# One image's scan moved into the sampling stage of a four-layer convolution kernel, 448 columns at a time

## The reference, cut to what matters

```python
# third layer: deformable convolution, 9 taps, 4 corners each
py = base_y + kh + dy;  px = base_x + kw + dx          # dy, dx from a 3x3 convolution
y0 = floor(py); x0 = floor(px); wy = py - y0; wx = px - x0
sampled = v00*(1-wy)*(1-wx) + v01*(1-wy)*wx + v10*wy*(1-wx) + v11*wy*wx   # v: gathered pixels
sampled = sampled * mask
out = einsum('bkhwc,ock->bohw', sampled, w2)

# fourth layer: selective scan over the pixels of an image, 128 channels, 16 states
def step(h, inp):
    dt_t, B_t, C_t, u_t = inp
    dA = exp(dt_t[..., None] * A)
    h = dA * h + (dt_t * u_t)[..., None] * B_t[:, None, :]
    return (h, einsum('bdn,bn->bd', h, C_t))
```

## Time and profile before

| | us |
|---|---|
| median of 3 runs | 6257.39 |
| lowest and highest run | 6249.47 to 6259.31 |
| span of the profiled execution, first to last instruction | 6244.6 |
| the median stands over that span by | 12.8 |
| busy PE / DVE / ACT / POOL in the span | 4411.3 / 5012.8 / 2533.4 / 4904.1 |
| sampling stage, first to last gather issue | 885.6 to 3119.0 |
| first memset of the scan stage | 3167.9 |
| mean granted TensorE clock, as a share of 2.4 GHz | 0.81 |

### The profile page before, as it was taken

The page is one execution under the profiler, slowest core; times in us unless marked ns, Lnnn a source line. Parts: engine busy times, 40 slices in busy tenths (PEclk is TensorE's granted clock), DMA queues, the critical chain, the costliest instruction groups (busy, mean ns, idle before and its releaser), DMA issues. The chain is left out here.

```text
span 6244.6 us, 55481 instructions
## 1 busy us (share of the span) xinstructions
PE 4411.3 (71%) x14922; PEld 2398.8 (38%) x14922; DVE 5012.8 (80%) x3958; ACT 2533.4 (41%) x3949; POOL 4904.1 (79%) x3492
## 2 busy tenths in 40 slices
PE   3777656565555657463338888888888888888887
PEld 1566523332323233232214444444444444444443
DVE  5899736776766676666639999999999999999998
ACT  2222111111111111110026666666766766766664
POOL 1777627777777777777719999999999999999997
PEclk8887766656565656655569999999999999999999
DMA  6666623444434443443324544454454544444443
GB/s 165 133 135 136 139 79 104 123 114 145 123 104 133 127 123 105 135 116 114 104 79 149 165 157 154 161 162 148 160 163 147 169 151 156 160 153 162 155 152 120
DMA packets 379240, 855.17 MB, mean 137 GB/s; under 512 B 195672, under 2 KB 238576, under 8 KB 374580
## 3 DMA queue, kind: packets, MB, share of 16 engines
q1 hardware_dynamic: 294228, 619.96, 33.3%
q0 software_dynamic: 84672, 231.32, 12.4%
HBM read 768.83 MB, written 56.48 MB: 132 GB/s over the span
## 5 line engine op out<-in xcount | busy, mean ns | idle before, releaser
L863 POOL DMA_INDIRECT fl_quad<-table,fl_idx x1764 | 1697.3, 962 | 695.0 <-issue 536.7
L2097 POOL TENSOR_TENSOR ma_hc<-ma_h,ma_cc 128x784 f32<-128x784 f32 x1024 | 1882.2, 1848 | 235.8 <-DVE ma_h L1998 203.7
L1642 PE MATMUL ma_bank<-ma_hc,ident 128*128 128x392 f32 x4096 | 1528.0, 495 | 10.2 <-POOL ma_hc L2097 7.6
L1998 DVE TENSOR_TENSOR_SCAN ma_h<-ma_da,ma_state,ma_bank 128x784 f32<-128x784 f32 x768 | 1418.0, 1846 | 101.6 <-DVE ma_bank L1985 3.5
L1014 DVE TENSOR_TENSOR fl_part<-fl_quad,fl_bank 128x2304 f32<-128x2304 f32 x196 | 500.1, 2552 | 710.1 <-DMA fl_quad<-table,fl_idx 696.6
L1867 ACT ACTIVATE ma_da<-ma_dt,ma_a_neg 128x784 f32<-128x784 f32 x1024 | 948.2, 943 | 271.1 <-DVE ma_h L1998 176.6
L1985 DVE TENSOR_TENSOR ma_bank<-ma_dtu,ma_bank 128x784 f32<-128x784 f32 x1024 | 983.4, 960 | 80.5 <-PE ma_bank L1629 79.1
L1155 PE MATMUL fl_bank<-ident,fl_tap 128*128 128x128 f32 (+1 forms) x980 | 242.3, 409 | 937.4 <-DVE xres L1032 876.0
L1642 PEld LDWEIGHTS ma_bank<-ma_hc,ident 128*128 128x128 f32 x4096 | 705.3, 189 | 449.5 <-POOL ma_hc L2097 36.0
L1022 DVE TENSOR_REDUCE fl_tap<-fl_part 128x576 f32<-128x2304 f32 x196 | 796.5, 4064 | 0.1
L1629 PE MATMUL ma_bank<-ma_bc,ma_sel 96*128 96x512 bf16 (+1 forms) x2048 | 514.8, 333 | 376.2 <-DVE ma_h L1998 361.0
(11 more groups left out here) (229 smaller groups left out, 6131.6 us busy)
## 6 DMA issues: line engine op xcount, KB each, us to landing
ma_cc<-c_rows SPq DMA_DIRECT2D x512, 784.0 KB, 4.3
mx_win<-flat SPq DMA_DIRECT2D x64, 878.0 KB, 10.3
fl_quad<-table,fl_idx POOLq DMA_INDIRECT x1764, 2.7
table<-fl_xt SPq DMA_DIRECT2D x64, 392.0 KB
mx_mask<-in_c_mask SPq DMA_DIRECT2D x56, 294.0 KB, 4.5
ma_xs<-ma_x SPq DMA_DIRECT2D x64, 196.8 KB, 5.6
ma_xs<-ma_x SPq DMA_DIRECT2D x64, 196.5 KB, 6.1
mx_xf<-flat SPq DMA_DIRECT2D x8, 816.0 KB, 15.8
```

The lines of the kernel that those rows point to most:

```text
L863: gp.indirect_dma_start(quad[i][:, kk, :], None, table, bass.IndirectOffsetOnAxis(ap=idx[i][:, kk:kk + 1], axis=0))\
L1642: ins = pe.matmul(ps_y[:, t, :], ident[:], hc[:, n % RH, at], start=False, stop=(n == DS - 1))
L1998: dve.tensor_tensor_scan(h[:, i % RH, :], da[:, i % RH, :], ps_bu[i % 2], before, ALU.mult, ALU.add).then_inc(scand, 1)
L2097: gp.tensor_tensor(hc[:, i % RH, :], h[:, i % RH, :], cc[:, i % (NGRP * GRP), :], ALU.mult)\
```

## The change

Image 0's fourth layer leaves the scan stage, which now goes through seven images (`NLITE` = 1, `NBM` = `NB - NLITE`), and is done inside the sampling stage. It is cut into 7 pieces of 448 columns, which with the two branches make 14 sections (`NSECT`) of 16 units, 224 units. `units(T)` gives slot T its units: none before `FIRST` = 59, then 5 units in 3 slots (`RATE`), so one or two in a slot, up to slot 193. GpSimd does none of it: `times_c` is now VectorE's, and C is spread by TensorE into PSUM (`spread_c`), as B is. Beside the units run a section's preparation and output (`chain`), on TensorE, ScalarE and VectorE, and before the first unit `set_up` (slot 3) and `intro` (slots 54 to 58).

Room is made for it. `RQ` is 3, `part` is one buffer and not two, `xres` holds two pairs and not four, and in PSUM convolution chunks, offset chunks and transposes share one bank (`cps`, `xps`, `tps`), so each waits until the one before was read; `turn_x` moves behind `turn_offsets`. `stage_norm3` is gone: `normal` takes each pair's statistics in the first slots of the next pair, and the last pair's behind the last tile. The weights of the scan are loaded in this stage by 26 more transfers on SP's queue. The tensor_reduce over the corners (`corners`) is as before, on all tiles.

```diff
@@ constants
+NLITE = 1
+LC = 448
+NLC = PIX // LC
@@ stage_flow
-    RQ = 4
+    RQ = 3
+    NSECT = 2 * NLC * NLITE
+    NUNIT = DS * NSECT
+    INTRO = NSEQ + 5
+    PERSLOT = 3
+    NINTRO = 13
+    FIRST = INTRO + (NINTRO + PERSLOT - 1) // PERSLOT
+    RATE = (5, 3)
...
-        part = [s_.sb(f"part{i}", [TS, 4, K2, CH]) for i in range(2)]
+        part = s_.sb("part", [TS, 4, K2, CH])
...
-        cps = [bank[:, 4 + i, :] for i in range(2)]
-        xps = bank[0:2 * PW, 6, 0:7 * CH].rearrange("p (a c) -> p a c", c=CH)
-        tps = bank[:, 7, 0:HT * M].rearrange("p (a m) -> p a m", m=M)
+        cps = bank[:, 2, :]
+        xps = bank[0:2 * PW, 2, 0:7 * CH].rearrange("p (a c) -> p a c", c=CH)
+        tps = bank[:, 2, 0:HT * M].rearrange("p (a m) -> p a m", m=M)
+        cof = bank[:, 3, 0:4 * K2]
+        ps_b, ps_c, ps_y, ps_f = (bank[:, 4 + i, 0:LC] for i in range(4))
...
+        def units(T):
+            lo, hi = ((T + i - FIRST) * RATE[0] // RATE[1] for i in range(2))
+            return list(range(max(lo, 0), min(hi, NUNIT)))
@@ VectorE
             def tile(T):
...
+                own = units(T)
+                if own:
+                    times_b(own[0])
+                    scan(own[0])
                 scale(T)
+                if own:
+                    times_c(own[0])
+                    chain(own[0])
+                if own[1:]:
+                    times_b(own[1])
                 if T + RQ < NTILE:
-                    pick(T + RQ)
+                    take(T + RQ)
                 corners(T)
+                if own[1:]:
+                    scan(own[1])
                 if T:
                     add(T - 1)
+                if own[1:]:
+                    times_c(own[1])
+                    chain(own[1])
@@ TensorE
             def free(q, r, h, c):
-                if r == 0 and c < 2:
+                if r == 0 and c == 0:
                     if b:
-                        pe.wait_ge(biased, START + 7 * b)
+                        pe.wait_ge(xcopied, START + 4 * b)
                 elif r == 0:
-                    pe.wait_ge(grown, START + 7 * b + c - 1)
-                elif c < 2:
+                    pe.wait_ge(grown, START + 7 * b + c)
+                elif c == 0:
                     pe.wait_ge(grown, START + 7 * b + 7)
                 else:
-                    pe.wait_ge(biased, START + 7 * b + c - 1)
+                    pe.wait_ge(biased, START + 7 * b + c)
...
+            def spread_b(V):
+                S, n = divmod(V, DS)
+                if n == 0:
+                    pe.wait_ge(l_low, START + S + 1)
+                pe.wait_ge(l_scand, START + V)
+                pe.matmul(ps_b, sel[:, n, :], lbc[S % 2][:], start=True, stop=True).then_inc(l_bready, 1)
+
+            def spread_c(V):
+                S, n = divmod(V, DS)
+                pe.wait_ge(l_hcd, START + V)
+                pe.matmul(ps_c, sel[:, DS + n, :], lbc[S % 2][:], start=True, stop=True).then_inc(l_cready, 1)
+
+            def gather_y(V):
...
+                pe.wait_ge(l_hcd, START + V + 1)
+                pe.matmul(ps_y, ident[:], lhc[V % 2][:], start=False, stop=(n == DS - 1)).then_inc(l_yd, 1)
+
+            def after_scan(V):
+                if V + 1 < NUNIT:
+                    spread_b(V + 1)
+                chain(V)
+
+            def after_c(V):
+                gather_y(V)
+                if V + 1 < NUNIT:
+                    spread_c(V + 1)
...
             def tile(T):
+                own = units(T)
+                before = units(T - 1)
                 if T:
                     project(T - 1)
+                if before:
+                    after_c(before[-1])
+                if own:
+                    after_scan(own[0])
+                if own[1:]:
+                    after_c(own[0])
                 turn(T)
+                if own[1:]:
+                    after_scan(own[1])
@@ stage_mamba
-    NCHUNK = NQ * NB
+    NBM = NB - NLITE
+    NCHUNK = NQ * NBM
```

More of the change, by code:

```diff
@@ L787, in padded_rows @@
+        for half in (lower, upper):
+            loads += [(vec[half, 3:4], "m_gamma"), (vec[half, 4:5], "m_beta"), (win[half, :], "m_win"),
+                      (vec[half, 5:6], "m_b_p"), (wp[half, half], "m_wp")]
+        NL = len(loads) + 3
+        NSET = 11
         def padded_rows(h):
@@ L838, in _ @@
                             sp.dma_start(dst, zero[0:HH, :].rearrange("p (b c) -> p b c", b=2)).then_inc(bordered, 16)
+            sp.wait_ge(l_zeroed, START + 1)
+            for dst, name in loads:
+                sp.dma_start(dst, k[name]).then_inc(l_consts, 16)
+            sp.dma_start(wt4[:].rearrange("p j d -> p (j d)"), k["m_conv_w"].partition_broadcast(P))\
+              .then_inc(l_consts, 16)
+            for half, name in ((lower, "m_s1"), (upper, "m_s2")):
+                sp.dma_start(vec[half, 7:8], k[name].partition_broadcast(CH)).then_inc(l_consts, 16)
             store_table(0)
@@ L1171, in tile @@
                 turn(T)
+                if own[1:]:
+                    after_scan(own[1])
             pe.wait_ge(consts, START + 16 * (NLOAD + 1))
-            program(add_up, prepare, tile)
+            program(add_up, prepare, tile, normal, set_up, intro)
             project(NTILE - 1)
+            if units(NTILE - 1):
+                after_c(units(NTILE - 1)[-1])
+            out(NCK - 1)
+            out_average(NCK - 1)
+            out_last(NCK - 1)
+            for s in range(4):
+                normal(NPAIR - 1, s)
@@ new lines, in intro @@
+            def intro(i):
+                if i in (3, 6):
+                    affine(i // 3 - 1)
+                if i in (0, 3):
+                    keep(i // 3)
+                if i in (1, 4):
+                    root_in(i // 3)
+                if i == 6:
+                    take_u(0)
+                if i == 7:
+                    silu(0)
+                if i == 8:
+                    soft(0)
+                if i == 9:
+                    high(0)
+                if i == 11:
+                    mid(0)
+                if i == 12:
+                    for V in range(2):
+                        decay(V)
@@ L1257, in tile @@
             def tile(T):
-                e = T % 2
+                e, own = T % 2, units(T)
                 if T == 0:
                     spread_coef(0)
+                if own:
+                    unit(own[0])
                 if T + 1 < NTILE:
@@ L1263, in tile @@
                     spread_coef(T + 1)
+                if own:
+                    chain(own[0])
+                if own[1:]:
+                    unit(own[1])
                 act.wait_ge(turned, START + T + 1)
```

691 lines of the change are left out of this document (579 added, 112 removed).

## The result

The changed kernel takes 6573.4 us (median of four runs, 6558.9 to 6580.5) against 6254.7 us: 1.051 times the time before, 95% interval 1.049 to 1.052. The forecast was slower at 6347 us, in a range up to 6470. The sign was right; the size was not, and the time lies outside the range.

What follows compares the result with a forecast made beforehand. GpSimd's issue of gathers was taken to bound the sampling stage at 11.40 us a tile, with VectorE some 700 us free. The terms -370, -6, +18, +8, +95 and +344 sum to +89, giving 6347 us, range 6180 to 6470.

Steps and rivals of the forecast that it cites:

- -370: Scan stage: one image of eight leaves, 260 VectorE instructions, 370 us less.
- -6: Between sampling and scan stages: the small stage goes, last statistics, output and stage change remain; 6 us less, ends +5 and -12.
- +18: Before the scan starts: one PSUM bank for convolutions, offset products and x transposes makes engines wait, 18 us more.
- +8: Scan set-up, slots 54 to 58: VectorE waits some 5 us a slot where 4.2 are free, 8 us more.
- +95: Sampling stage: VectorE's own work, 1639 us against GpSimd's 1532, becomes the bound; less 12 at the end, 95 us more.
- +344: Sampling stage from slot 59: VectorE waits before times_c for TensorE's copy of C, 344 us more, ends 0 and about 480.
- the walk: TensorE's slot, followed from the end of tensor_reduce: C comes at 9.1 to 13.8 us in convolution and two-offset-product slots.
- Rival 2: TensorE mostly at the lower clock in the sampling stage: 480 us of VectorE waiting, 6483 us; chance 0.17.
- Rival 1: TensorE's clock stays up at 2.4 GHz in the sampling stage: 192 us of waiting, 6195 us; chance 0.19.
- Rival 3: VectorE's waits are covered: 6003 us with its own work as only bound, 5908 at GpSimd's pace; chance 0.06.
- Rival 4: Section's chain holds the samples' copies back on ScalarE: up to 5 us a section, 70 more, 6417 us; chance 0.09.

Runs made afterwards that it cites:

- late_conv: The changed kernel with TensorE issuing gather_y and C's copy before prepared work and project, convolutions before the next turn, and VectorE's addition before the second scan: 6168.5 us.
- warm1: The changed kernel with four more fp32 products of 448 columns, results unused, on TensorE in front of turn in slots with units: 6411.8 us, ratio 1.026.
- late_warm: late_conv with the four unused TensorE products of warm1 in front of turn: 6227.4 us, ratio 0.997.

## Why the prediction was wrong in size, point by point

The spans differ by 322.9 us (6567.5 and 6244.6), and the terms forecast +89.

- **-370, an image less in the scan stage: right.** The stage takes 2707.4 us for 3076.7, -369.3.
- **-6, the end of the sampling stage: right.** 26.4 us for 33.5 from the last addition to the scan stage's first memset, -7.1.
- **+18 before the first tile: +28.6.** The bank's part was right: 0.77 us before each of six convolutions, 1.8 before six offset products, 4 us at the x transposes, some 20 in all. Missing were 8.7 us before the first convolution (784.5 against 775.8 us), 4.2 of them a longer change of stage, some 3 a somewhat later end of the stage ahead, and 1.3 three memsets.
- **+8 for the set-up in slots 54 to 58: +29.** The forecast had VectorE wait for ScalarE and TensorE some 5 us a slot. It waited 10.27 and 11.28 us for the square root's activation (L1764) in two convolution slots, and 10.8 for project in a third: the section's first steps stand behind the prepared work as C does. late_conv bears this out in part: with the convolution products moved, the two waits are 4.8 and 7.0 us, and slots 54 to 58 take 75.0 us for 85.3. The rest of the +29 no run took apart. VectorE's rows after the change:

```profile
1565.55 0.63 DVE L1237 TENSOR_TENSOR fl_l<-fl_l,fl_lt 128x448 f32<-128x448 f32 x1 [10.27 <-ACT fl_lt L1764]
...
1585.04 0.63 DVE L1237 TENSOR_TENSOR fl_l<-fl_l,fl_lt 128x448 f32<-128x448 f32 x1 [11.28 <-ACT fl_lt L1764]
...
1610.82 0.28 DVE L1182 TENSOR_TENSOR fl_xres<-fl_bank,fl_xres 64x128 f32<-64x128 f32 x1 [10.82 <-PE fl_bank L1484]
```

- **+95, VectorE's own work: right.** 1612.65 us busy in the stretch for 1639 forecast; a unit is 0.624 + 1.141 + 0.620 = 2.39 us for 2.34. Slots 0 to 53 ran as before (+1.1 us).
- **+344, VectorE's waits: 540 in the same stretch. This is the step that failed**, by 196 of the 234 us that the forecast was short. The mechanism was the one named. What was too small is the time at which C comes, in the walk through TensorE's slot:

| wait for C (B at the end) | forecast | measured |
|---|---|---|
| 28 convolution slots | 3.6 each, 101 | 5.5, 153 |
| 15 slots with two offset products | 7.6, 114 | 9.9, 148 |
| 15 with one, or turning offsets | 52 | 71 |
| last 22 slots | 1.0, 22 | 1.7, 37 |
| the other 55 | 1.0, 55 | 1.3, 69 |
| wait for B, all slots | 0 | 62 |

The wait for B is no error of its own. 58 of its 62 us lie in slots in which C comes late as well; VectorE would have spent them waiting for C. So the two together measure how late C is.

In the convolution slots C's copy ends 12.5 us behind the tensor_reduce on average; the walk had 10.4 with two units and 9.1 with one. In the slots with two offset products it is 16.4 for 13.8 and 12.5. Three of the walk's entries were too short:

- *The clock at the start of a slot.* TensorE idles 4.6 us before turn on average, and turn runs at the lower level (1.30 us) in 122 of the 135 slots. The convolution product behind it takes 6.4 us on average (5.4 to 7.2) for the 5.3 taken. With two offset products turn, project and gather_y are at the lower level in all 15 slots. The mean clock rose in these slots, from 0.58 to 0.66, and the part of the slot that VectorE waits for was still mostly the slow one.
- *gather_y.* It takes 1.0 us at the upper level and 1.86 at the lower, for 0.8 and 1.5.
- *The section's own products*, for which the walk had a few tenths of a us in a convolution slot and nothing elsewhere. In 28 of the slots that wait for C they stand ahead of its copy, and they account for 71 us of waiting at most (an estimate: in each of these slots the shorter of the wait and the products). One of the longest waits is this one of 12.04 us, with eight products for the next section (L1524) ahead of the convolution:

```profile
1949.98 1.30 PE L1474 MATMUL fl_bank<-ident,fl_tap 128*128 128x128 f32 x5 [4.84 <-DVE fl_xres L1182]
1951.07 0.58 PE L1566 MATMUL fl_bank<-fl_lbc,fl_sel 96*128 96x448 bf16 x1
1951.58 6.34 PE L1524 MATMUL fl_bank<-fl_l,fl_wt 64*128 64x448 f32 x8
1957.85 4.54 PE L686 MATMUL fl_bank<-fl_xp,fl_cw 128*64 128x448 f32 x6
...
1968.15 0.62 DVE L1303 TENSOR_TENSOR fl_lhc<-fl_lh,fl_bank 128x448 f32<-128x448 f32 x1 [12.04 <-PE fl_bank L1571]
```

No run splits the 196 us between these. warm1 shows what a clock of 0.85 gives back, 168 us of waiting; but that is counted from the measured clock and not from the mix of levels that the walk took. No run moved the section's products alone.

Rival 2, "mostly at the lower clock", with its 480 us of waiting and 6483 us, was the nearer case, and had 0.17. That its waiting is so near the 540 is luck in part: it has everything at the lower level, where project and gather_y ran at the upper one in all 28 convolution slots, and it is still 60 us short, since it too had next to nothing for the section's products. Rival 1 (the clock stays up) fell: 0.66. By the Trainium skill ("TensorE: Matmul & The Clock Gate", on the clock gate) activity lifts the clock. The trace agrees with that in warm1 and late_warm, where added products took it to 0.85 and 0.87; the products of this change took it only from 0.58 to 0.66. Rival 3 needed an order in which C does not come last; late_conv shows that such an order exists, 405 us under the change, though 165 over the 6003 named. Rival 4 fell: it would show as TensorE waiting for the samples' copies, and in the stretch TensorE waits 28.8 us for them, at most 0.83 at a time, against 50.6 in the same slots before.

Four slips in the working change nothing of this. In the earlier trace rows GpSimd's digit is 2 in slice 6, in which the stage opens, and 7 from slice 7 on. A scan with a product's fixed part (0.14 us) is 1.115 us and not 1.15. With a bias addition VectorE wants C at 7.5 us and not 7.3, which makes the 3.6 us of a convolution slot a little too long. The sum is 6346.4 and not 6347.

## What to carry to other kernels

When idle time of one engine is filled with a chain that goes to and fro between two engines, the time is set by the order in the other engine's queue: put first what the waiting engine needs first, and everything that only has to be done some time (a convolution, a projection) into the stretch in which that engine would idle. A second buffer without a new order of the rest moves more than half of the wait to the next instruction (262 of 478 us here). Take the durations of such a walk at the clock that the engine has just behind its idle stretch, not at the stage's mean. And count in it every product that can stand ahead in the queue, those of the new chain too.

## What the runs showed of the hardware that was not expected

- A VectorE product with both operands in SBUF holds up a GpSimd gather that starts inside it: 2.43 us for 0.95, until the product is done. With the small operand in PSUM both run freely, at the same 2.55 us. The mean gather went from 0.962 to 1.128 us (row below, 900 to 3100 us) and the kernel before from 6247 to 6534. The Trainium skill has a rule on this ("SBUF — State Buffer", "Who interferes with whom"): a VectorE instruction with two SBUF inputs contends with a GpSimd instruction that reads SBUF. The trace agrees in one direction: all 195 gathers that start inside a product are held up, while 194 products that start inside a gather take 2.56 us as always, and that gather 0.945. A gather has its indices (`fl_idx`) in SBUF; that it is this read which is held up no run shows.

```profile
L863 POOL DMA_INDIRECT fl_quad<-table,fl_idx x1536 | 1732.8, 1128 | 467.9 <-issue 467.9
```

- A higher granted clock of TensorE can go with a longer time: 0.87 and 6227 us in late_warm, 0.71 and 6169 in late_conv.
